# The rests and low parts of the weighted rows of both halves of a super, taken in one Vector operation each

## The reference, cut to what matters

```python
e = x_l[src] + x_r[dst] + (ea @ W_e).reshape(-1, H, C)
e = jnp.where(e > 0, e, NEG_SLOPE * e)
logits = jnp.einsum('ehc,hc->eh', e, att)
m = jax.ops.segment_max(logits, dst, num_segments=N)
a = jnp.exp(logits - m[dst])
denom = jax.ops.segment_sum(a, dst, num_segments=N)
alpha = a / denom[dst]
out = jax.ops.segment_sum(x_l[src] * alpha[..., None], dst, num_segments=N)
```

## Time and profile before

| what | us |
|---|---|
| median of 3 runs (2901.64 to 2909.39) | 2902.66 |
| the profiled execution, its own time | 2907.21 |
| its span, first to last instruction | 2905.1 |
| the attention loop, first L1978 to last L1978 | 1475.2 to 2449.8 |

### The profile page before, as it was taken

One profiled execution on the slowest core, in us unless ns is written; L12 is line 12 of the kernel. 1 busy time (PEld: TensorE's weight loads), 2 busy tenths in 40 slices (PEclk: granted clock), 3 DMA queues, 4 the chain that ended last, 5 costly groups with the idle time before them and its releaser, 6 DMA issues. The chain is left out here.

```text
span 2905.1 us, 58320 instructions
## 1 busy us (share of the span) xinstructions
PE 2278.8 (78%) x15227; PEld 1706.2 (59%) x15227; DVE 2061.7 (71%) x8090; ACT 1214.2 (42%) x4032; POOL 1530.8 (53%) x1526
## 2 busy tenths in 40 slices
PE   5996667777773799609089999999999998349994
PEld 3774233333331466405079999999999997326663
DVE  8775777666655411169069999999999998675445
ACT  1663100000001222114068888888888887721110
POOL 1234777777777777767654444444444441004441
PEclk8786775666556899859589999999999998568997
DMA  5401333533362435124033333233333333251224
GB/s 180 133 22 34 91 96 95 151 103 100 99 93 70 123 108 151 54 52 156 21 83 75 73 75 75 73 75 75 73 75 74 74 72 69 96 205 58 66 62 151
DMA packets 260534, 262.08 MB, mean 90 GB/s; under 512 B 145587, under 2 KB 213005, under 8 KB 259842
## 3 DMA queue, kind: packets, MB, share of 16 engines
q0 software_dynamic: 63808, 147.58, 19.3%
q1 hardware_dynamic: 188370, 103.29, 12.7%
q10 hardware_dynamic: 8048, 7.57, 0.8%
HBM read 196.23 MB, written 62.07 MB: 89 GB/s over the span
## 5 line engine op out<-in xcount | busy, mean ns | idle before, releaser
L1834 POOL DMA_INDIRECT l_rows<-xl_tab,l_ra x440 | 461.7, 1049 | 502.2 <-DMA l_ra<-rec_a 396.7
L966 PE MATMUL c_ps<-room_a 128*128 128x256 f32 x864 | 429.4, 608 | 176.2 <-DVE room_a L1093 85.3
L945 POOL DMA_INDIRECT room_a<-h_tab,c_rec x432 | 453.5, 1050 | 135.0 <-issue 96.0
L856 POOL DMA_INDIRECT rec_a<-room_a x390 | 382.3, 980 | 119.2 <-issue 117.7
L966 PEld LDWEIGHTS c_ps<-room_a 128*128 128x128 f32 x864 | 193.8, 274 | 411.8 <-DVE room_a L1093 270.3
L1978 DVE CUSTOM_DVE_ANT_0 l_junk<-l_ps_lb,l_pen 128x256 bf16<-128x256 f32 x880 | 319.0, 418 | 6.3 <-PE l_ps_lb L1940 4.4
L1100 DVE TENSOR_TENSOR x_sb<-x_sb,c_ps 128x256 f32 x432 | 181.7, 421 | 181.5 <-PE c_ps L966 169.1
L1897 PE MATMUL l_bank_l<-g_att_d,l_rz 128*128 128x4 f32 x1760 | 238.3, 256 | 5.2 <-ACT l_rz L1884 3.1
L1872 ACT ACTIVATE l_val<-l_rows,l_val 128x64 f32<-128x64 f32 x880 | 234.1, 337 | 7.1
L1862 ACT ACTIVATE g_acc<-g_acc,l_cexp x880 | 233.9, 345 | 1.2 <-issue 1.2
L1897 PEld LDWEIGHTS l_bank_l<-g_att_d,l_rz 128*128 128x128 f32 x1760 | 219.3, 191 | 22.1 <-ACT l_rz L1884 7.5
(11 more groups left out here) (526 smaller groups left out, 5685.5 us busy)
## 6 DMA issues: line engine op xcount, KB each, us to landing
m_w<-in_L_ffn_w SPq DMA_DIRECT2D x16, 1024.0 KB, 7.9
rec_a<-p_blank SPq DMA_DIRECT2D x110, 102.0 KB
l_ra<-rec_a SPq DMA_DIRECT2D x220, 51.0 KB, 2.1
e_w<-in_L_ffn_W SPq DMA_DIRECT2D x16, 512.0 KB, 10.2
l_rows<-xl_tab,l_ra POOLq DMA_INDIRECT x440
room_a<-h_tab,c_rec POOLq DMA_INDIRECT x432, 2.8
xrr_tab<-q_xrr SPq DMA_DIRECT2D x25, 256.0 KB, 2.6
f_xrr<-xrr_tab SPq DMA_DIRECT2D x5, 1280.0 KB, 13.7
```

Source lines behind the costliest of these rows:

```text
L856: pool.indirect_dma_start(K["rec_a"], bass.IndirectOffsetOnAxis(ap=K["stage_i"][:, u, k:k + 1], axis=0), K["stage_r"][:, u, k, :], None).t ...
L945: pool.indirect_dma_start(rows[:, u, :], None, K["h_tab"], bass.IndirectOffsetOnAxis(ap=rec[:, n % RSLOTS, k, 0:1].bitcast(I32), axis=0)). ...
L966: pe.matmul(ps[s % NB][:, :], hot[:, u, :], rows[:, u, :], start=True, stop=True).then_inc(s_agg, 1)
L1834: pool.indirect_dma_start(rows[:, u, j, :], None, K["xl_tab"], bass.IndirectOffsetOnAxis(ap=ra[:, u, j, A_SRC:A_SRC + 1].bitcast(I32), axi ...
```

## The change

In the DVE program of `attend` the two `rest` operations of 260 elements become one of 520, and so do the two `low` operations. The wait for `val1` (ACT's half) therefore stands ahead of the one `rest` operation, together with the wait for `val`, where before it stood between the two halves. The semaphores `rest` and `low` are raised once for a super, and PE's wait for `low` counts accordingly. PE's, ACT's, POOL's and SP's instructions stay as they are.

```diff
@@ PE
-                    pe.wait_ge(S["low"], SUB * r + SUB)
+                    pe.wait_ge(S["low"], r + 1)
@@ DVE
                 if on4:
-                    whole = [val[:, v4 % 2, j, :, :].rearrange("p h c -> p (h c)") for j in range(SUB)]
-                    some = [rest[:, v4 % 2, j, :] for j in range(SUB)]
+                    whole = val[:, v4 % 2, :, :, :].rearrange("p j h c -> p (j h c)")
+                    some = rest[:, v4 % 2, :, :].rearrange("p j c -> p (j c)")
                     dve.wait_ge(S["val"], r4 + 1)
-                    for j in range(SUB):
-                        if j == SUB - 1:
-                            dve.wait_ge(S["val1"], r4 + 1)
-                        dve.tensor_tensor(some[j], whole[j], uppers(whole[j]), ALU.subtract).then_inc(S["rest"], 1)
+                    dve.wait_ge(S["val1"], r4 + 1)
+                    dve.tensor_tensor(some, whole, uppers(whole), ALU.subtract).then_inc(S["rest"], 1)
...
                 if on4:
-                    for j in range(SUB):
-                        dve.wait_ge(S["rest"], SUB * r4 + j + 1)
-                        dve.tensor_tensor(low[:, v4 % 2, j, :], some[j], uppers(some[j]), ALU.subtract
-                                          ).then_inc(S["low"], 1)
+                    dve.wait_ge(S["rest"], r4 + 1)
+                    dve.tensor_tensor(low[:, v4 % 2, :, :].rearrange("p j c -> p (j c)"), some, uppers(some), ALU.subtract
+                                      ).then_inc(S["low"], 1)
```

## The result

The changed kernel takes 2928.33 us (median of 6 runs, 2922.0 to 2931.89) against 2903.57 for the kernel before in the same comparison: a ratio of 1.0085, 95% interval [1.0071, 1.0099]. It is slower by 25 us. The forecast was 2908 with a range up to 2920 and "within 0.3%" as the likeliest outcome. So the range missed and the direction of the lean held.

A forecast was written before the change was run, and what follows sets the result against it. DVE was taken to bound the attention loop, with PE close behind. Saving -31 us, `low` waiting for `rest` +9 and `rest` waiting for ACT +27 summed to +5 us: 2908 us, range 2896 to 2920.

The forecast's parts named there:

- The bound and the mechanism: Attention loop: DVE sets the pace; merged `rest` waits for ACT's half, `low` for all of `rest`, and nothing fills the hole.
- the second of those added: DVE's merged `rest` waits for ACT's last weighted row: 0.13 us a turn, +27 us over 220 supers.
- The two other terms: On DVE, two merges save 0.14 us a turn (-31 us); `low` waiting for the whole of `rest` adds 0.04 (+9).
- The second rival: At DVE's `rest`, a longer hand-over from ACT, 0.17 us rather than 0.05: +29 us, 2932; chance 0.10.
- Its row, 0.17 at L1978: Evidence for a long hand-over: ACT's L1852 ends at 1816.21, the DVE maximum said to wait starts 0.17 us later.
- its sign: In the profile afterwards, a gap of 0.2 us or more ahead of DVE's `rest` would show the second rival.
- The first rival: At DVE's `rest`, no wait for ACT; PE, with a 0.07 us hole, becomes the bound: -15 us, 2888; chance 0.10.
- PE's cover: PE's L1910 loads at 1909.92, `low` with hand-over is there by 1909.87, so PE's wait for `low` costs nothing.

The follow-up runs named there:

- e3: The kernel before, four operations of 260 elements, with ACT's half taken first in `rest` and `low`: 2936.58 us, ratio 1.0107.
- e4: The changed kernel with `arg` moved ahead of the four maxima, its second part after the first maximum: 2875.93 us, ratio 0.9896.
- e5: The kernel before, all four operations of 260 elements, with `arg` moved ahead of the maxima as in e4: 2890.22 us, ratio 0.9957.
- e1: The changed kernel with the two waits ahead of the merged `rest` in the other order, `val1` written first: 2917.62 us, ratio 1.0035.
- e2: The changed kernel with a no-operation taking the wait for `val`, so the merged `rest` carries only that for `val1`: 2916.73 us, ratio 1.0042.
- e7: The kernel before with only the two `rest` operations merged, waits written as in the changed kernel: 2942.49 us, ratio 1.0127.
- e10: e4 with the first part of `arg` for the next super put between `rest` and `low`: 2886.35 us, ratio 0.9945.
- e6: The kernel before with only the two `low` operations merged, `rest` left in two: 2899.84 us, ratio 0.9983.
- e8: e4 with the sum into the accumulator moved from ahead of `mlow` to between `rest` and `low`: 2919.0 us, ratio 1.0041.
- e9: e4 with the two waits ahead of `rest` in the order of e1: 2876.0 us, ratio 0.9914.

## Why the prediction was wrong, point by point

**The bound and the mechanism were right.** DVE sets the pace; `rest` waits for ACT's half, nothing stands behind it that could fill the hole, and `low` waits for the end of `rest`. e3, e4 and e5 show that the wait for ACT decides the sign: with the wait and no merge +31 us, with the merge and no wait a gain of 17 in the loop over the same order unmerged.

**The term that failed is the second of those added, the wait for ACT's half.** It was put at 0.13 us a turn, with a hand-over of 0.05 and bounds of 0.02 and 0.05. It is 0.19, with a hand-over of 0.10 to 0.11; `rest` starts 1909.64 - 1908.02 = 1.62 after `arg` where 1.56 was forecast. The bounds came from the earlier trace rows, where the operation that waits carries the wait for ACT itself; in the changed kernel that wait is on an instruction ahead of it. e1 puts it back on the operation, and the wait is 0.20 - 0.07 = 0.13, the figure of the prediction. The order was to be read from the print of DVE's queue before the result, where `m_yp` stands ahead of `m_hc`; what it costs was not. The error is 0.06 x 219 = 13 us of the 20 between 5 and 25.

**The two other terms were each a little kind.** The merged operations take 0.62 from start to start and not 0.61, so the pair of merges saves 0.12 a turn and not 0.14: 4 us. `low` waits 0.05 and not 0.04: 2 us. By turn: -0.12 + 0.05 + 0.19 = +0.12, beside the loop's mean of +0.113.

**The second rival came nearest, at too small a chance, too high a price and with another reason.** It named a longer hand-over, from 0.06 on, and that came. Its reason was that an instruction starts late from an emptied queue. In e1 and e2 the queue is as empty and `rest` starts after 0.03 to 0.04, so that reason falls; what counts is where the last wait stands. Its row, 0.17 at L1978, has that form: the waits stand on an instruction of their own ahead of the maximum. I set it aside as a price for each turn because it occurs once in 178 us. It isn't a clean price either, since the same wait elsewhere is followed by 0.51 us in the kernel before and by 0.39 in the changed one. The rival had 0.10 of the chance. The prediction would have taken a gap of 0.2 for its sign and 0.13 for the forecast's; 0.19 is all but the former.

**The first rival did not come.** `rest` did wait. Its price was wrong too: PE's hole was 0.15 and not 0.07 (e4), so PE would not have become the bound at -15 us. The rule of the Trainium skill ("Perfetto Trace Analysis", section "Optimizing Scalar/DVE Operations") that grouping can help where the engine is saturated, by an estimated 26 us here, is borne out only where the later input is early: e4 against e5 has 17 us. Where it is late, the same grouping loses 25.

**PE's cover was used up, at no cost.** The prediction left 0.05 between the hand-over of `low` and L1910's start. The wait for ACT is 0.06 longer than forecast, and L1910 then waits some 0.02 for `low` in nearly every turn. PE doesn't set the pace there, so it costs nothing; in e5, e7 and e10 L1910 waits 0.08 to 0.10, and in e10 that wait is part of what sets the turn. The price of `low`'s wait and the gain of the merge by itself were confirmed by e6 (-4 us where -5 was forecast).

## What to carry to other kernels

Before two operations are merged, ask when each input of the merged one is ready: the first of the two was hiding the wait of the second, and that cover goes. Where an operation waits for two semaphores, put the one that comes last on the operation itself; in this program that meant writing its wait first (e1). If the merge is wanted, first move the producer's input forward until the wait is gone, then merge; and look up who else waits for what is moved past.

## What the runs showed of the hardware

- A DVE operation started 0.03 to 0.04 us after the end of the ACT operation that it waited for when it carried the wait itself (e1, e2, e3), and 0.10 to 0.11 after it when that wait was written as the later of two (the changed kernel, e7, e8), which by e1 and e2 puts it on an instruction ahead. When neither had to be waited for, both orders cost nothing (e4, e9).
- An f32 DVE operation on two inputs of 520 elements took 0.70 us and 0.62 from start to start, against 0.42 and 0.34 for 260.
- PE's weight load of L1897 started 0.02 us after the start of the load ahead of it where it waited for nothing (e4), though that load's record is 0.10 long.
